# Windowed attention of a two-layer kernel: one joint projection by tokens, turned afterwards, with the maxima written into the token buffer

## The reference, cut to what matters

```
h = layernorm(x) * (1 + scale_a) + shift_a
q = h @ Wq.T      # 16 heads of 16
k = h @ Wk.T      # 4 heads of 16, each shared by 4 query heads
v = h @ Wv.T      # 4 heads of 16
s = q k / sqrt(16), keys within 128 tokens of the query on either side
x = x + gate_a * (softmax(s) @ v) @ Wo.T
```

## Time and profile before

| | |
|---|---|
| median of 3 executions | 3681.88 us (3681.81 to 3682.46) |
| the profiled execution | 3681.08 us |
| its span in the profile | 3679.3 us |
| PE busy, whole program | 3321.7 us, 90% |
| DVE, ACT, POOL busy | 53%, 43%, 15% |
| windowed attention, first to last instruction | about 1328 to 2025 us of the span |

### The profile page before, as it was taken

How to read it: one execution, slowest core, us unless ns; L and a number is a source line. 1 busy time by engine, 2 the same in 40 slices (tenths; PEclk the granted TensorE clock), 3 DMA queues, 4 the chain that set the end, 5 groups by cost and what they waited for, 6 DMA issues and landing times. The chain is left out here.

```text
span 3679.3 us, 47577 instructions
## 1 busy us (share of the span) xinstructions
PE 3321.7 (90%) x16112; PEld 1955.1 (53%) x16113; DVE 1945.8 (53%) x4733; ACT 1564.9 (43%) x3481; POOL 567.7 (15%) x591
## 2 busy tenths in 40 slices
PE   5999996785999969999998899998899899997998
PEld 3455554453666644444443566666445566665454
DVE  1999994332111125555553677776331677775332
ACT  1766662220222215555554565665221456554211
POOL 0000001543000048100000322221000211111112
PEclk8999997887999979999999999999899999998999
DMA  3000003102111121000000100000000100000000
GB/s 128 1 1 1 1 1 121 46 23 97 46 46 46 44 60 55 9 1 1 1 1 1 60 10 10 9 8 5 24 0 1 36 8 10 9 8 5 12 12 23
DMA packets 72640, 90.19 MB, mean 25 GB/s; under 512 B 10975, under 2 KB 61427, under 8 KB 72179
## 3 DMA queue, kind: packets, MB, share of 16 engines
q1 hardware_dynamic: 65186, 69.28, 5.7%
q0 software_dynamic: 7248, 18.26, 1.6%
HBM read 59.63 MB, written 24.12 MB: 23 GB/s over the span
## 5 line engine op out<-in xcount | busy, mean ns | idle before, releaser
L1602 DVE CUSTOM_DVE_ANT_0 sb_win_masked<-ps_win_pss,sb_win_around 128x384 f32<-128x384 f32 (+1 forms) x512 | 255.7, 538 | 229.7 <-PE ps_win_pss L1709 229.7
L2010 ACT ACTIVATE sb_loc_pr<-ps_loc_psw,sb_loc_nb,sb_loc_sc 128x256 f32<-128x256 f32 x512 | 281.0, 568 | 187.8 <-DVE sb_loc_nb L2137 187.8
L2213 PE MATMUL ps_loc_psa<-sb_stk_w,sb_loc_hT 128*128 128x512 f32 x768 | 350.8, 607 | 4.9 <-DMA sb_stk_wo<-in_loc_wo 3.2
L2500 PE MATMUL ps_mlp_ps<-sb_mlp_hT,sb_stk_w 128*128 128x512 f32 (+1 forms) x768 | 322.7, 613 | 22.3 <-DVE sb_mlp_hid L2453 22.3
L1527 ACT ACTIVATE sb_win_pT<-ps_win_pst 128x512 f32<-128x512 f32 x368 | 199.7, 595 | 207.0 <-PE ps_win_pst L1720 205.4
L2213 PEld LDWEIGHTS ps_loc_psa<-sb_stk_w,sb_loc_hT 128*128 128x128 f32 x768 | 142.2, 192 | 181.8 <-issue 178.3
L2500 PEld LDWEIGHTS ps_mlp_ps<-sb_mlp_hT,sb_stk_w 128*128 128x128 f32 (+1 forms) x768 | 130.1, 184 | 201.7 <-issue 201.7
L719 PE MATMUL ps_rec_psp<-sb_rec_hT,sb_rec_w 128*128 128x512 f32 x512 | 235.7, 604 | 1.0 <-ACT sb_rec_hT L422 1.0
L2453 DVE SCALAR_TENSOR_TENSOR sb_mlp_hid<-ps_mlp_ps,sb_stk_col,sb_mlp_gl 128x512 f32<-128x512 f32 x96 | 71.7, 750 | 303.4 <-ACT sb_mlp_gl L2422 303.4
L2422 ACT ACTIVATE sb_mlp_gl<-ps_mlp_ps,sb_stk_col 128x512 f32<-128x512 f32 x96 | 65.9, 687 | 381.8 <-PE ps_mlp_ps L2500 381.6
L1709 PE MATMUL ps_win_pss<-sb_win_kT,sb_win_q 32*128 32x384 f32 (+1 forms) x1024 | 223.4, 518 | 4.7 <-DVE sb_win_top L1602 3.0
(11 more groups left out here) (316 smaller groups left out, 6552.8 us busy)
## 6 DMA issues: line engine op xcount, KB each, us to landing
sb_exp_rows<-sorted_tokens SPq DMA_DIRECT2D x72, 128.0 KB, 2.0
expert_results<-sb_exp_res SPq DMA_DIRECT2D x72, 128.0 KB, 1.7
sb_keep_x<-in_x SPq DMA_DIRECT2D x1, 4096.0 KB, 22.8
sb_moe_w_in<-in_L_ffn_w_in_eDF SPq DMA_DIRECT2D x8, 512.0 KB, 11.3
sb_moe_w_sw<-in_L_ffn_w_swiglu_eDF SPq DMA_DIRECT2D x8, 512.0 KB, 11.4
sb_exp_w_out<-in_L_ffn_w_out_eFD SPq DMA_DIRECT2D x8, 512.0 KB, 7.6
sb_stk_angles<-in_angles SPq DMA_DIRECT2D x32, 128.0 KB, 3.8
out_y<-sb_stk_y SPq DMA_DIRECT2D x8, 512.0 KB, 2.9
```

The costliest lines, as they stand in the source:

```text
L1602: i = nc.vector.tensor_tensor_reduce(masked[:, pair % 2, j, 0:keys], pss[:, (n + j) % PLAIN, 0:keys], around[:, first:first + keys], 1.0, ...
L2010: e = nc.scalar.activation(pr[:, hf, h], psw[:, hf, h // 2, h % 2 * 256:h % 2 * 256 + 256], ACT.Exp, scale=sc8[:, b, hh:hh + 1], bias=nb[: ...
L2213: t = nc.tensor.matmul(psa[:, c], hT[:, b, k, 1 - k:P + 1 - k], w[:, k, c * 512:(c + 1) * 512], start=(k == 0), stop=(k == KD - 1))
L2500: i = nc.tensor.matmul(ps[at:at + M, q % 2, i2], w1[:, k, i2 * HID + f * P:i2 * HID + f * P + M], hT[:, b, k], start=(k == 0), stop=(k == ...
```

## The change

The three weights become one, `wqkv`, with 256 + 64 + 64 = 384 columns and no padding. PE projects with the tokens as the stationary operand (`project`), so queries, keys and values all come out with tokens on partitions. ACT copies the queries into a padded token buffer `qtok` (`copy_tokens`), a ring of four tiles; DVE copies keys into `ktok` and values into `v` (`copy_key_tokens`). Then PE turns the queries (`turn_queries`, slot 5) and the keys (`turn_keys`, slot 6), and ACT and DVE copy them out of `psm` as before (`copy_queries`, now slot 5; `copy_keys`, now slot 6). The maxima go straight into column 16 of the token buffer, so when `turn_maxima` turns it a second time, it brings queries and maxima at once, and `place_maxima` is a copy. POOL fills the paddings at the start, and sets the maxima of a tile back to zero after their turn (`forget_maxima`). DVE's `divide` moves from slot 2 to slot 3.

```diff
@@ loads @@
-                sp.dma_start(wq[:], ...)
-                sp.dma_start(wk[:], ...)
-                sp.dma_start(wv[:], ...)
-                sp.dma_start(kbias[:], a["key_bias"]).then_inc(s_w, 16)
+                sp.dma_start(wqkv[:], a["att_wqkv"].rearrange("(k p) n -> p k n", p=P)).then_inc(s_w, 16)
@@ gpsimd @@
-                nc.gpsimd.memset(top[:], 0.0).then_inc(s_pad, 1)
+                nc.gpsimd.memset(qtok[:, 0:2], 0.0).then_inc(s_pad, 1)
+                nc.gpsimd.memset(ktok[:], 0.0).then_inc(s_pad, 1)
+                pool.wait_ge(s_pad, 2)
+                nc.gpsimd.memset(ktok[:, :, :, AHD:AHD + 1], -1.0).then_inc(s_pad, 1)
...
+                nc.gpsimd.memset(qtok[:, 2:TOKENS], 0.0).then_inc(s_pad, 1)
                 nc.gpsimd.memset(v[:, :, :, 1], 1.0).then_inc(s_pad, 1)
+                def forget_maxima(u):
+                    pool.wait_ge(s_tt, u + 1)
+                    nc.gpsimd.memset(qtok[:, u % TOKENS, :, :, AHD:AHD + 1], 0.0).then_inc(s_zero, 1)
                 for u in range(2, NT):
                     combine(u)
                     if u + 2 < NT:
                         gather(u + 2)
+                    if u >= 6:
+                        forget_maxima(u - 6)
@@ scalar @@
+                def copy_tokens(u):
+                    act.wait_ge(s_proj, u + 1)
+                    if u >= TOKENS:
+                        act.wait_ge(s_tt, u - TOKENS + 1)
+                    nc.scalar.copy(qtok[:, u % TOKENS, :, :, 0:AHD],
+                                   psm[:, 0:D].rearrange("p (g c d) -> p g c d", g=AG, c=AKV)).then_inc(s_qtok, 1)
...
                         if k == 3 and s + 2 < NT:
+                            copy_tokens(s + 2)
+                        if k == 5 and s + 2 < NT:
                             copy_queries(s + 2)
                 deviation(0)
+                act.wait_ge(s_pad, 5)
@@ vector @@
+                def copy_key_tokens(u):
+                    dve.wait_ge(s_qtok, u + 1)
+                    if u >= 2:
+                        dve.wait_ge(s_kp, u - 1)
+                    nc.vector.tensor_copy(ktok[:, u % 2, :, 0:AHD], ...).then_inc(s_ktok, 1)
+                    nc.vector.tensor_copy(v[:, u, :, 0], ...).then_inc(s_v, 1)
...
-                                                           top[:, u % 2, g, lane:lane + 1])
+                                                           qtok[:, u % TOKENS, g, c + j, AHD:AHD + 1])
...
-                        if k == 2 and 0 <= s - 2 < NT:
+                        if k == 3 and 0 <= s - 2 < NT:
                             divide(s - 2)
+                        if k == 3 and s + 2 < NT:
+                            copy_key_tokens(s + 2)
...
-                        if k == 5 and s + 2 < NT:
+                        if k == 6 and s + 2 < NT:
                             copy_keys(s + 2)
@@ tensor @@
-                def project_queries(u): ...
-                def project_keys(u): ...
+                def project(u):
+                    pe.wait_ge(s_hT, u + 1)
+                    if u >= 4:
+                        pe.wait_ge(s_logs, u - 3)
+                    for k in range(KD):
+                        i = nc.tensor.matmul(psm[:, 0:QKV], hT[:, u % 2, k], wqkv[:, k], start=(k == 0), stop=(k == KD - 1))
+                    i.then_inc(s_proj, 1)
+                def turn_queries(u):
+                    pe.wait_ge(s_qtok, u + 1)
+                    pe.wait_ge(s_v, u + 1)
+                    if u >= TOKENS:
+                        pe.wait_ge(s_zero, u - TOKENS + 1)
+                        pe.wait_ge(s_x, u - 3)
+                    for g in range(AG):
+                        i = nc.tensor.transpose(psm[:, g * P:(g + 1) * P], qtok[:, u % TOKENS, g]..., ident[:])
+                    i.then_inc(s_qp, 1)
+                def turn_keys(u):
+                    pe.wait_ge(s_ktok, u + 1)
+                    pe.wait_ge(s_q, u + 1)
+                    nc.tensor.transpose(psm[:, 0:P], ktok[:, u % 2]..., ident[:]).then_inc(s_kp, 1)
...
                 def project_out(u):
-                        pe.wait_ge(s_q, u + 5)
+                        pe.wait_ge(s_qtok, u + 5)
+                        pe.wait_ge(s_v, u + 5)
```

More of the change, by code:

```diff
@@ L1406, in windowed_attention @@
         psm = m.ps("psm", [P, 512])
-        (s_w, s_pad, s_wog, s_sum, s_gated, s_in, s_st, s_mv, s_ln, s_rstd, s_nmr, s_xn, s_tr, s_hT, s_qp, s_q, s_kvp,
-         s_k, s_v, s_s, s_top, s_tt, s_qm, s_sT, s_e, s_pv, s_raw, s_share, s_logs, s_inv, s_oT, s_out, s_x) = (
-            m.sem(n) for n in ("w_in pad gated_wo sum gated in stats mv lnv rstd nmr xn tr hT qp q kvp k v scores top topT "
+        (s_w, s_pad, s_wog, s_sum, s_gated, s_in, s_st, s_mv, s_ln, s_rstd, s_nmr, s_xn, s_tr, s_hT, s_proj, s_qtok, s_ktok, s_qp, s_q, s_kp,
+         s_k, s_v, s_zero, s_s, s_top, s_tt, s_qm, s_sT, s_e, s_pv, s_raw, s_share, s_logs, s_inv, s_oT, s_out, s_x) = (
+            m.sem(n) for n in ("w_in pad gated_wo sum gated in stats mv lnv rstd nmr xn tr hT proj qtok ktok qp q kp k v zero scores top topT "
                                "qm scoresT exp pv raw share logs inv oT out xadd").split())
@@ L1483, in _ @@
                         gather(u + 2)
+                    if u >= 6:
+                        forget_maxima(u - 6)
+                for u in range(NT - 6, NT - TOKENS):
+                    forget_maxima(u)
             @block.scalar
@@ L1724, in turn_maxima @@
                     pe.wait_ge(s_top, (u + 1) * AH // 2)
-                    if u + 2 < NT:
-                        pe.wait_ge(s_v, u + 3)
-                    else:
+                    pe.wait_ge(s_k, min(u + 3, NT))
+                    if u >= 2:
                         pe.wait_ge(s_x, u - 1)
                     for g in range(AG):
-                        i = nc.tensor.transpose(psm[:, g * P:(g + 1) * P], top[:, u % 2, g], ident[:])
+                        i = nc.tensor.transpose(psm[:, g * P:(g + 1) * P], qtok[:, u % TOKENS, g].rearrange("p c d -> p (c d)"),
+                                                ident[:])
                     i.then_inc(s_tt, 1)
@@ L2630, in lay_out @@
     out["keepmask"] = (np.arange(BLK) % CHUNK != 0).astype(np.float32)
-    wq = np.zeros((D, AG, AKV, 32), np.float32)
-    wq[..., 0:AHD] = np.asarray(inputs["L1_attn_Wq"]).T.reshape(D, AKV, AG, AHD).transpose(0, 2, 1, 3)
-    out["att_wq"] = wq.reshape(D, AG * P)
-    wk = np.zeros((D, AKV, 32), np.float32)
-    wk[..., 0:AHD] = np.asarray(inputs["L1_attn_Wk"]).T.reshape(D, AKV, AHD)
-    out["att_wk"] = wk.reshape(D, P)
-    out["att_wv"] = c(np.asarray(inputs["L1_attn_Wv"]).T)
+    wq = np.asarray(inputs["L1_attn_Wq"]).T.reshape(D, AKV, AG, AHD).transpose(0, 2, 1, 3).reshape(D, D)
+    out["att_wqkv"] = c(np.concatenate((wq, np.asarray(inputs["L1_attn_Wk"]).T, np.asarray(inputs["L1_attn_Wv"]).T), axis=1))
     wo = np.zeros((AG, AKV, 32, D), np.float32)
```

65 lines of the change are left out of this document (25 added, 40 removed).

## The result

| | before | after |
|---|---|---|
| median of 11 executions each | 3681.81 us | 3674.89 us (3673.83 to 3676.59) |
| profiled execution | 3681.08 us | 3675.25 us |
| span | 3679.3 us | 3673.4 us |
| one full step of the stage | 20.45 us | 20.19 us |
| PE busy in it | 19.93 us | 19.47 us |

What follows compares the result with a forecast made beforehand. PE's queue, in program order, was taken to bound the windowed attention. Full steps -10.7, three short steps -0.6 and the start -0.3 made -11.6 us, from 3681.88 to 3670.3 us; range 3660 to 3679.

Steps and rivals of the forecast that it cites:

- The mechanism: Windowed attention: PE's queue sets the time, but ACT's exponentials hold slots at least 1.3 us apart, 1.55 with masks.
- The third rival: Behind slot 5: masks could start on the bank freed first, winning 10.4 us more, for 3660 us; chance 0.12.
- The predicted idle gap: Behind slot 5, before the masks: PE's saved 0.4 us becomes idle time and gains nothing.
- The projection: Slot 3 to slot 4: four joint passes take 1.42 us instead of 1.98, gaining 0.56 us (0.49 to 0.66).
- The turn of the keys: Behind slot 6: one turn of 0.145 us on PE, losing 0.15 us a step (0.1 to 0.3).
- The short steps: Steps 1, 16 and 17, whose turned scores end at slot 5: 0.2 us gained each, 0.6 together.
- The start: Start of the stage: 1.1 us lost and 1.4 gained, together -0.3 us, between +2 and -2.
- The 1.1 us of later start: Before PE's first turn: ACT's first normalisation waits for five fills, moving that turn from 1347.99 to 1349.1.
- The first steps: First three projections, at half clock: 0.4 us gained twice and 0.6 in the third.
- The cover at the output projection: Behind slot 4: copies end at about 2.3 us, slot 4 issues until 2.49, leaving 0.2 us before PE would wait.
- The second rival: Output projection: slower copies bring 0.2 to 0.3 us of new waiting 26 times, 3675 to 3679 us; chance 0.15.
- The clock: PE in every step: turns and idleness behind slot 5 lower its clock, 1.65 us a fall, 3713 us; chance 0.09.

## Why the prediction was right, point by point

**The mechanism held.** For the steady steps, PE's queue bounds the stage, only slot 3 to 4 gained, and the 0.4 us saved behind slot 5 came to nothing (1.55 us before and after). Three runs show it: work put there was free, work moved there was worth 0.42 us a step, and shorter exponentials opened it. The third rival (the exponentials don't bind) is refuted by these. The predicted idle gap of some 0.4 us is there (0.44), though the view shows 0.18 of it as idle.

**The size was off**: the forecast was a gain of 11.6 us, the medians differ by 6.9. That lies inside the range, by its width and not by the sum, and at 3674.89 us just above the 3674.5 under which the prediction called the result faster, with a chance of 0.78; the interval of the ratio still excludes no change. A full step gained 0.26 us instead of 0.41, so over steps 3 to 29 6.9 us came where 0.41 in 25 full steps and the two short ones make 10.65. Two terms are mis-sized. The projection was put at 1.42 us by a line through passes of 128 and 256 columns; it took 1.48. That line has no price for a group; a pass is 0.32 us, and the group carries 0.19 (1.48 = 4 x 0.32 + 0.19; the output projection fits nearly, 8 passes at two thirds of 0.32 and 0.19 make 1.90 of its 1.92, while the old query projection's 16 passes are 0.08 us off). It was inside my bounds of 1.32 to 1.49, at their end. The turn of the keys was put at 0.145 us, a quarter of a group of four, and took 0.26 where it stood alone; with masks a little shorter the place lost 0.23 (I had 0.15, bounds 0.1 to 0.3). In both I carried a group's time per pass or per turn over to a shorter group, which hides what a group costs once.

**The short steps.** Taken as 0.2 us of gain each: step 16 gained 0.13, step 17 0.34; step 1 can't be read because of the clock.

**The start.** Up to the first turn of maxima the sum had -0.3 us: 1.1 lost at the first turn, 1.4 gained in the first projections. Measured in the two traces: 0.56 gained and 0.54 lost, 0.0 together. Both terms were wrong by more than 1.6 us and cancelled, so that part of the agreement is luck. Steps 1 and 2, for which the sum had a gain of 0.6, lost 1.16. The 1.1 us of later start didn't come. The fill did delay ACT, whose first normalisation now starts at 1347.10 and not at 1340.11:

```profile
1347.10 0.60 ACT L1509 ACTIVATE sb_win_xn<-sb_keep_x,sb_win_nmr,sb_win_rstd 128x256 f32<-128x256 f32 x1 [8.53 <-POOL sb_win_v L1479]
```

But POOL's first sum started 6.13 us after its first gather instead of 7.86, right behind the fills, where it had waited 2.1 us for the gather. That less weight is loaded at that moment (384 KB instead of 704) is the likely cause; it was not tried by itself. The first steps were put at a gain of 1.4 and lost 0.5: four turns at the low clock take 1.09 us, for which the sum had no term, and the two hand-overs about 1.0 and 0.8 us of idle PE. The clock itself differed too: in the kernel before it rose to 1.00 at the end of each of the first two projections, at 1353 and 1363, and fell again before the next; in the changed kernel it stayed at 0.50 until about 1375. It did rise in between in the second execution of the changed kernel, 5 us after the first turn, and didn't in the kernel before with moved values, so this isn't shown to be the change's. Steps 1 and 2 differ by 2.7 us between two executions of one program, so a loss of 1.16 there can't be put down to the change.

**The cover at the output projection** was forecast at 0.2 us and is 0.20, since the copies and the end of slot 4 both came 0.06 later, with the projection. The second rival didn't come about: ACT's copy takes 0.37 us in this layout. **The clock** stayed at 1.00 in all steps from 3 to 29, with five turns and an idle gap more in each, so that rival is refuted for the steady steps. The Trainium skill (TensorE: Matmul & The Clock Gate, Part 4: PE-mode transpose) says that a transpose doesn't count as busy the same way; no loss from it appeared in these steps, and no run here has turns without products beside them, so whether turns count stays open. POOL is held to PE's pace as expected; the waits of the stage show it, and nothing waits for it:

```profile
POOL sb_win_qtok L1484 <- PE ps_win_psm L1757: 421.8, 27, 20.1
```

The two profiled executions differ by 5.8 us; the interval of the ratio (4 to 10 us) holds both.

## What to carry to other kernels

Before costing an operation that is taken out of the bounding engine's queue, look for a place where the program already runs without it: the time from slot to slot there is the floor, and only what is above it can be won. If the removed work stood at such a floor, move other work of the same engine into the gap; here that was worth more (0.42 us a step) than the change itself (0.26). Price a group of matrix products as a fixed part and a part per pass, from two groups of different length, and never as a quarter of four. Mind also what stands behind a group: here one turn cost 0.26 us ahead of products of another shape and 0.16 ahead of products of its own.

## What the runs showed that I had not expected

- A group of fp32 passes between scores (whose products take 32 rows each) carries about 0.19 us (projection) or 0.15 us (turns) once, beside 0.32 us a pass of 384 columns and 0.11 us a turn. Between the values and the masks instead of between scores and values a single turn costs 0.16 us, not 0.26.
- The values' products, which write to different groups of 32 partitions, overlap so fully that two heads' cost as much as four heads' (0.98 against 1.00 us).
- A copy that only moves 512 columns from PSUM costs DVE as much as the addition it replaced: 687 against 686 ns.
- With the clock at its lower level for part of a stage's start, the first two steps differ by 2.7 us between executions of one program, and step 1 takes from 16.3 to 22.3 us among close relatives.
